# A hybrid attention and expert block: side work of the first attention regrouped, routing partly on GpSimd, throwaway matmuls at the start

## The reference

```python
x = x + linear_attention(layernorm(x))     # 16 heads of 8
x = x + ffn(layernorm(x))
x = x + softmax_attention(layernorm(x))    # 16 heads of 8
x = x + ffn(layernorm(x))

# linear_attention: phi = elu + 1 of q and k; S and z run over the sequence (causal)
S = S + pk[..., :, None] * v[..., None, :];  z = z + pk
num = einsum('bhd,bhde->bhe', pq, S);  den = sum(pq * z) + 1e-5;  out = num / den

# ffn: 16 experts in 4 groups, 2 shared ones
scores = sigmoid(x @ router_w.T);  s = scores + bias
group_score = top_k(s per group, 2).sum();  the best 2 groups stay, the others are masked
topk_idx = top_k(masked s, 4);  tw = 2.5 * scores[topk_idx] / (their sum + 1e-20)
y = einsum over all experts of (silu(x@gate) * (x@up)) @ down, weighted by tw, + shared experts
```

## Time and profile before

| | us |
|---|---|
| three runs | 577.60, 577.95, 577.96 |
| median | 577.95 |
| the profiled execution | 574.57 |
| its span in the profile | 572.8 |

### The profile page before, as it was taken

One profiled execution on the slowest core, in us unless ns is written; L12 is line 12 of the kernel. 1 busy time (PEld: TensorE's weight loads), 2 busy tenths in 40 slices (PEclk: granted clock), 3 DMA queues, 4 the chain that ended last, 5 costly groups with the idle time before them and its releaser, 6 DMA issues. The chain is left out here.

```text
span 572.8 us, 11532 instructions
## 1 busy us (share of the span) xinstructions
PE 517.6 (90%) x3757; PEld 390.4 (68%) x3757; DVE 432.7 (76%) x1105; ACT 344.8 (60%) x607; POOL 290.0 (51%) x276
## 2 busy tenths in 40 slices
PE   3878887899999999999788898988999999999996
PEld 3555564577888888888454555645678888888884
DVE  3678798569798898567677887989479796886663
ACT  3676746456555655666457767676865655555553
POOL 4765572146666756777421305020166656666664
PEclk9799988899999999999779999999999999999999
DMA  6358870213454344235641524310442444354340
GB/s 168 114 185 263 245 249 2 72 62 98 107 116 127 92 119 121 98 112 180 200 117 51 185 75 143 116 39 3 62 106 97 109 135 124 103 137 132 95 143 20
DMA packets 48549, 67.60 MB, mean 118 GB/s; under 512 B 6625, under 2 KB 18930, under 8 KB 48498
## 3 DMA queue, kind: packets, MB, share of 16 engines
q1 hardware_dynamic: 45392, 66.47, 39.9%
q10 hardware_dynamic: 3106, 0.48, 0.5%
HBM read 53.56 MB, written 13.37 MB: 117 GB/s over the span
## 5 line engine op out<-in xcount | busy, mean ns | idle before, releaser
L639 POOL TENSOR_TENSOR KS<-PT,QS 128x512 fp32r<-128x512 f32 x144 | 186.2, 1294 | 118.1 <-ACT QS L836 106.1
L831 ACT ACTIVATE bank<-bank 128x512 f32<-128x512 f32 x128 | 74.5, 582 | 98.5 <-PE bank L856 97.9
L1562 DVE TENSOR_TENSOR PT<-CS,bank 128x512 f32<-128x512 f32 x128 | 87.4, 683 | 45.1 <-PE bank L856 44.3
L854 PE MATMUL bank<-XH,WH 128*128 128x512 f32 (+1 forms) x288 | 115.4, 401 | 1.7 <-DVE PT L1434 1.5
L856 PE MATMUL bank<-XH,WL 128*128 128x512 f32 (+1 forms) x288 | 112.9, 392 | 0.0
L855 PE MATMUL bank<-XL,WH 128*128 128x512 f32 (+1 forms) x288 | 112.6, 391 | 0.0
L836 ACT ACTIVATE QS<-PT 128x512 fp32r<-128x512 f32 x144 | 90.1, 626 | 12.2 <-DVE PT L1567 11.8
L1458 DVE TENSOR_REDUCE MEXP<-bank 128x4 f32<-128x1024 f32 x64 | 78.2, 1223 | 22.8 <-PE bank L966 22.1
L1567 DVE TENSOR_TENSOR PT<-PT,bank 128x512 f32<-128x512 f32 x128 | 88.0, 687 | 9.5 <-ACT bank L831 1.6
L750 ACT ACTIVATE PT<-bank 128x1024 f32<-128x1024 f32 x64 | 65.6, 1025 | 40.1 <-PE bank L998 39.8
L1021 PE MATMUL bank<-PT,V 128*32 128x256 f32 (+1 forms) x1024 | 64.6, 372 | 0.3 <-ACT OTS L760 0.3
(11 more groups left out here) (185 smaller groups left out, 770.6 us busy)
## 6 DMA issues: line engine op xcount, KB each, us to landing
CS<-combine_rows SPq DMA_DIRECT2D x128, 256.0 KB, 3.2
head_rows<-HP SPq DMA_DIRECT2D x28, 256.0 KB, 3.0
QS<-head_rows SPq DMA_DIRECT2D x28, 256.0 KB, 2.7
KS<-head_rows SPq DMA_DIRECT2D x28, 256.0 KB, 3.0
head_rows<-PHI SPq DMA_DIRECT2D x14, 256.0 KB, 3.1
out_dram<-X SPq DMA_DIRECT2D x4, 256.0 KB, 3.7
stage<-in_L_ffn_gate_w_dram SPq DMA_DIRECT2D x5, 192.0 KB, 3.8
stage<-in_L_ffn_up_w_dram SPq DMA_DIRECT2D x5, 192.0 KB, 4.0
```

The lines of the kernel that those rows point to most:

```text
L639: pool.tensor_tensor(GL[:, (u - 1) % 3, :], GG[:, (u - 1) % 3, :], GH[:, (u - 1) % 3, :].bitcast(f32), ALU.subtract).then_inc(F.gl, 1)
L831: act.activation(TH[:, u, :] if u < SHARED else G[u % 3][:, :], G[u % 3][:, :], ACT.Silu).then_inc(F.th, 1)
L854: pe.matmul(out, wh, vh, start=start, stop=False)
L1562: dve.tensor_tensor(ab, CS[:, e % CBUFS, :], U[u % 3][:, :], ALU.mult).then_inc(F.b, 1)
```

## The change

- PE gets 22 throwaway 128x128 matmuls: 12 before the first transposes, 2, 1 and 1 behind the three groups of transposes, and 6 behind the value product of chunk 0 (slot 2).
- The keys of the first head group are multiplied on DVE instead of POOL. The norm statistics of chunk 1 move into DVE's prologue, those of chunk 2 to slot 2, and its other steps one slot earlier; the features of chunk 1 move from slots 5 and 6 to 4 and 5.
- The 6 weight pieces become 18 copies and 18 subtractions of 384 columns, behind the block copies of their slot on ACT; so do the features' steps on ACT.
- The epsilon of the denominator is a bias of ACT's copy `OTS`, with which `DEN` on DVE goes.
- Routing is split. DVE keeps the 8-way maxima, the replacements and the sum; its pairwise top-2 becomes 16 maxima. POOL does the rest, nine two-input steps, two compares and two fillers.
- Two of the four tiles `XN` in front of the experts go from ACT to POOL in both attentions.
- Slot 35 (first attention) and slot 36 (second) come before the first expert unit instead of behind it.

```diff
-        PIECE_SLOTS = [9, 11, 16, 18, 24, 26]
-        ROUTE_SLOTS = [{24: (0,), 25: (1,), 26: (2,), 27: (3,), 28: (4,), 29: (5,), 30: (6,), 31: (7,)},
...
-        NORM0_STATS = {1: 1, 4: 2, 8: 3}
-        NORM0_POWER = {2: 1, 5: 2, 9: 3}
+        PIECE_SLOTS = [9, 10, 10, 11, 11, 12, 15, 15, 17, 17, 19, 19, 23, 23, 25, 25, 27, 27]
+        POOL_ROUTE_SLOTS = [{24: (0,), 25: (2,), 27: (3,), 29: (5,), 30: (7,)},
...
+        DVE_ROUTE_SLOTS = [{25: (1,), 26: (2, 3), 28: (4, 5), 30: (6,)},
...
+        NORM0_STATS = {2: 2, 8: 3}
+        NORM0_POWER = {1: 1, 5: 2, 9: 3}
...
-        UNIT_SLOT = [35, 36]
+        UNIT_SLOT = [36, 37]
...
...
+            def route(A, c, part):
...
+                if part == 0:
+                    pool.wait_ge(A.th, c + 1)
+                    link(1, pool.tensor_tensor(T4[:, :, :], TH64[:, bass.ds(c * CT, CT), :], HALF[:, 0:1].unsqueeze(2)
+                                               .broadcast_to([P, CT, EXPERTS]), ALU.mult))
...
+                if part == 2:
+                    after(4)
+                    link(5, pool.tensor_tensor(GE[:, :, 0:GROUPS], TOP[:, :, 0].rearrange("p (t g) -> p t g", g=GROUPS),
+                                               TOP[:, :, 1].rearrange("p (t g) -> p t g", g=GROUPS), ALU.add))
...
+                if part == 5:
+                    after(12)
+                    pool.tensor_tensor(pool_junk[:, :], NEG[:, 0:1], NEG[:, 0:1], ALU.mult)
+                    link(13, pool.tensor_scalar(W[:, :, :], ER[:, :, 0:EXPERTS], -BIG / 3, None, ALU.is_lt))
...
             def scale_and_shift(L, c):
...
+                if c:
+                    pool.wait_ge(L.xt, c)
+                for t in range(CT // 2, CT):
+                    i = pool.tensor_scalar(XN[:, t, :], X[:, c * CT + t, :], MV[:, t, 0:1], RS[:, t:t + 1],
+                                           ALU.subtract, ALU.mult)
+                i.then_inc(L.xn, 1)
...
+                            act.activation(OTS[:, :], OT[:, :], ACT.Identity, bias=SUM_EPS[:, 0:1]).then_inc(A.ot, 1)
...
-                if k == 0 and n in PIECE_SLOTS:
-                    p = PIECE_SLOTS.index(n)
-                    act.wait_ge(s_raw[p % 2], 48 * (p // 2 + 1 + (p == PIECES - 1)))
-                    act.activation(flat(WH[:, UPP * p:UPP * (p + 1), :, :]), flat(stage[:, p % 2, :, :, :]),
-                                   ACT.Copy).then_inc(s_wh, 1)
...
-                    elif n - 1 in FEATURE_SLOT:
-                        features(*FEATURE_SLOT[n - 1])
...
                         full_blocks(1, n - 3)
                         full_blocks(0, n - 3)
+                    if n >= 2 and n - 1 in FEATURE_SLOT:
+                        features(*FEATURE_SLOT[n - 1])
+                    high_weights()
...
-                    for t in range(CT):
+                    for t in range(CT // 2):
                         i = act.activation(XN[:, t, :], X[:, (c - 2) * CT + t, :], ACT.Identity,
...
+            def keep_busy(times):
+
+                for _ in range(times):
+                    pe.matmul(BANK[1][:, 0:P], ident[:, :], ident[:, :], start=True, stop=True)
+
             pe.wait_ge(s_id, 2)
+            keep_busy(12)
...
                         values(0, c, PJ)
+                        if c == 0:
+                            keep_busy(6)
...
+                if part == 1:
...
+                    for t in range(CT * GROUPS):
+                        i = dve.max(out=TOP[:, t, :], in_=SB8[:, t, :])
...
-                        dve.tensor_scalar(DEN[:, :, :], o[:, :, :, HD], DEN_EPS, None, ALU.add).then_inc(A.dn, 1)
...
+                        if n == 1:
+                            dve.wait_ge(A.ph, 2)
+                            dve.tensor_scalar(KX[:, 0, :], PK, HEADS[:, 0:1], None, ALU.mult).then_inc(s_w0, 1)
```

More of the change, by code:

```diff
@@ L630, in slot @@
                                        ALU.subtract).then_inc(Lnext.xl, 1)
+                for part in POOL_ROUTE_SLOTS[k].get(n, ()):
+                    route(A, 0, part)
             def unit(k, c, u, cur, prev, more):
@@ L651, in unit @@
                                        ALU.subtract).then_inc(LN[2].xl, 1)
+                if more:
+                    for part in POOL_ROUTE_AT[prev].get(u, ()):
+                        route(AT[k], c + 1, part)
             layers(pool, slot, unit)
@@ L1580, in unit @@
                 if more:
-                    for part in ROUTE_AT[prev].get(u, ()):
+                    for part in DVE_ROUTE_AT[prev].get(u, ()):
                         route(AT[k], c + 1, part)
```

211 lines of the change are left out of this document (115 added, 96 removed).

## The result

The changed kernel takes 574.11 us in the median of 9 runs (571.2 to 576.02). The kernel before, measured beside it, takes 577.6 (9 runs, 576.31 to 578.75). The ratio is 0.9952, with a 95% interval of 0.993 to 0.9975: about 0.5% faster, 2.8 us by the ratio. The forecast was 11.6 us, and its range ended at 573.5. The sign was right, the size was not. The profiled execution has a span of 571.9 us (572.8 before).

The account below looks back on a forecast made before the run. PE was taken as the bound, full in the experts, with gaps in both attentions and the passage. Terms -3.6 + 0 - 2.5 - 1.5 - 2.5 - 1.5 = -11.6 us, from the median 577.95 to 566.4; range 560.0 to 573.5.

Parts of the forecast that it names:

- First chunk with the start: 15.8 to 41.9 us: later first scores +0.7, full clock -2.3, no wait for rows -1.5, weight copies -0.5; together -3.6.
- one of the moved side steps stays in them: First slots of the first chunk: two slots go no lower than 3.6 us, with one side step left; full clock gives -2.3.
- The wait for rows: First scores of the second chunk: features run one slot earlier, so the 1.50 us wait on rows from memory goes, -1.5.
- Second chunk: 41.9 to 62.1 us: faster slots only lengthen the wait for rows at its end; 0, bounds -0.6 and +0.8.
- rival A: Second to fourth chunk: scores wait for rows from memory and 4.75 of the 11.6 us are lost; 571.1 us, chance 0.20.
- Third chunk: 62.1 to 87.6 us: routing off DVE -2.6, normalization -0.8 on ACT, weight copies +0.6; taken as -2.5, bounds -4 and 0.
- Fourth chunk: 87.6 to 109.8 us: half the scaling leaves ACT, two weight copies come, DVE's routing shrinks; -1.5, bounds -4 and +0.5.
- Passage: 109.8 to 120 us: slot 35 before the first expert unit removes PE's 1.70 us wait; -2.5, bounds -3.5 and 0.
- rival E: Slots 25 to 32 and experts: DVE waits 1.3 us at each routing hand-over with POOL; about 577.9 us, chance 0.04.
- Rival D: Scalings before each chunk's transposes: POOL's tiles end last and are slower; at 3 us a tile 588 us, chance 0.08.
- Second attention: 300 to 405 us: two halved ACT scalings -0.5 each, smaller routing -0.5; -1.5, bounds -3 and +1.
- B: First slots and passage: PE is granted half speed again, losing the -2.3 and 1 us; 569.7 us, chance 0.14.

Follow-up runs that it names:

- queue_order: Changed kernel with the routing of the second 512 tokens, in the experts' first pass, shifted by a unit: 572.93 us, ratio 0.9913.
- no_throwaways: Changed kernel without its 22 throwaway matmuls, all else as changed: 576.64 us, ratio 0.9981.
- light_27_plain: Changed kernel with two VectorE side steps moved, ScalarE's table load and two weight copies out of slot 27, and no throwaway matmuls: 568.39 us, ratio 0.9802.

## Why the prediction was wrong, step by step

**First chunk with the start, -3.6 forecast, +1.6 and +0.4 in the two profiles.** Three steps failed. "Six cost 1.74 us" is too much: they took 1.50, and the first scores started at 15.54, because features and values ran at full pace 0.5 us earlier. That the clock stays at 2.4 GHz up to slot 5 ("so I expect 2.4 GHz there") was true in four of eight profiles. Worst is "one of the moved side steps stays in them": I named no row for the bias copy and the small subtraction, and asked of the lock of rows 6 only where it would go away. The steps that GpSimd now meets were to be looked up as well. The Trainium skill, page "SBUF — State Buffer", section "SBUF: two separate sides", names as VectorE's side of the lock its operations in a two-port mode, such as fp32 copies from SBUF to SBUF, and those with two SBUF inputs. The trace agrees: a copy with one SBUF input (1.86 us) and a subtraction with two (1.37) were stretched, while masked blocks that read a PSUM bank kept 1.27 beside GpSimd.

**The wait for rows, -1.5.** It went, and taken alone the moves earned 1.9 us at full clock. But ScalarE's 3.15 us of side work behind the wait came last: 1.05 us of pause at slot 12. The step that failed is that the 1.50 us "go": what stood in the cover of the wait was not added up.

**Second chunk, 0 forecast, +2.1.** The bounds (-0.6 to +0.8) were too narrow. 1.05 of it is that pause, and 0.84 a longer wait for rows at slot 19 (1.40, was 0.56), which is rival A in its mechanism. In the second profile that wait is 0.45, and half speed makes the chunk longer (5.2); why the wait has two lengths is open.

**Third chunk, -2.5 forecast, -4.3.** The sign held, the parts did not: routing 1.1 in place of 2.6, the scaling 0.8 as forecast, the weight copies up to 1.8 where I had a loss of 0.6. The rest I put down to the clock, 0.93 in this stretch before and 1.00 now; no run parts it. The sixteen maxima were stretched by nothing, as forecast, but they stand behind the statistics in one slot (from 83.43 on), and the masked blocks and scores wait for both:

```profile
84.64 0.17 DVE L1432 MAX8 TOP<-SB 128x8 f32<-128x8 f32 x1
...
84.72 1.12 DVE L1432 MAX8 TOP<-SB 128x8 f32<-128x8 f32 x15
85.76 1.27 DVE L1490 TENSOR_TENSOR PT<-bank,MASK 128x512 f32<-128x512 f32 x2
...
86.99 0.48 PE L1040 MATMUL bank<-QS,KS 24*128 24x256 f32 x4 [1.59 <-ACT PT L813]
```

**Fourth chunk, -1.5 forecast, +1.3 to +3.0.** Slot 27's pause stayed: I had counted "two new weight copies (1.0)" in that slot and still took a gain. Around the pause the clock was at half speed for some 10 us in the changed kernel and 3 before; with the pause gone the slots take 16.84 us. The fourth chunk's first scores started at 86.99 us, where the forecast had 81.5.

**Passage, -2.5.** -3.9, beyond the bound of -3.5. The mechanism was right: the pause of 1.70 us is gone, and the moved unit earns 2.0. The other 1.9 is not the moved unit: before the change the clock was at half speed here from 109.7 to 113.1, which accounts for up to 1.7 (an estimate, half of the 3.4 us), and in the changed kernel it was full.

**First expert network, 0 forecast, +1.5.** The forecast put the hand-overs between the engines at nothing here, and rival E priced them as all or nothing, with DVE as the one that waits. One of them, in the experts, cost 1.5 us, since GpSimd waited for DVE and behind its waiting addition stood work that PE needs. Rival D named that work (the tiles) but put the blame on their length; at 0.80 us a tile was below its limit of 0.82.

**Second attention, -1.5.** -0.8 and +0.7 in two profiles. In the sixteen profiles other than queue_order's it takes 143.4 to 148.6 us, by the clock: a gain of that size can't be seen there.

**The rivals.** B had 0.14 and two places, the first slots and the passage. Half speed came in several others, most of them near pauses that the change itself made or left, and its place differed between executions of one kernel. A, B and E each held in part, and their sum, not one of them, is the result. The 0.42 on all terms coming in together was too much: they rested on what stands next to a moved step, and I had looked that up for few of them. That the sign came out right owes something to the clock, which was full in the passage and the third chunk.

## What to carry to other kernels

When work moves, look up for each moved step what it now runs beside and what stands behind it, on every engine; a copy of 0.3 us next to a 1 us step of GpSimd cost more here than the routing earned. An instruction that waits for another engine belongs behind all work that something else waits for. The pauses of TensorE of 2.2 to 2.5 us in the attention cost their own length and came with some 3 to 10 us at half speed, so the long pauses come first. And one profile of a kernel is one draw of the clock: compare the lengths of two stretches only where both have the same granted clock.

## What the runs showed of the hardware

- VectorE, beside GpSimd operations of 1.03 us: a copy of a 1x128 row in two instructions 1.86 us (0.32 to 0.34 in the profiles where it stands elsewhere). Beside one of 1.26 us: a 128x128 subtraction 1.37 (0.28). A 128x512 product with one operand in PSUM, 0.66 to 0.69 us in either case, 1.27 to 1.29 for two.
- GpSimd: a 128x128 tile with two scalars 0.80 us, a 128x64 step with two inputs 0.29 to 0.32, a 128x16 sum 0.22.
- The granted clock can read 1.00 while TensorE works at the half-speed pace: in two profiles without the throwaway matmuls (no_throwaways, light_27_plain) five of the six matmuls of the features took 0.63 us each and the first 0.77, in a stretch that shows 1.00. In the kernel before, without them too, and in those with them they took 0.39 to 0.40 and the first 0.47 to 0.48. After 12 throwaway matmuls (4.71 us in all) the pace was full.
- Half speed near a pause: 8 of 8 profiles with 2.23 us in front of slot 7; 3 of 6 with 0.74 us there; 4 of 8 behind the 1.53 us before that; not in the one profile where the 2.23 us were filled with throwaway matmuls. In the first expert network, where TensorE was full before and behind, 3 of 13 profiles with a pause of 2.17 to 2.30 us. So the length of the pause alone did not decide.
